# A fused two-graph-layer kernel: its first two and its last three steps rearranged

## The reference, cut to what matters

```python
def reference(x, adj, ...):                      # x [16, 512, 256], adj [16, 512, 512], all float32
    h = maximum(layernorm(x), 0)
    # first graph layer (two hypergraph convolutions over H = (adj != 0)):
    #   conv(x, W, b) = Dn * (H @ (Be * (H^T @ (x @ W^T)))) + b
    #   r = relu(conv(h, W1, b1));  n = layernorm(r) * gamma + beta;  y = conv(n, W2, b2)
    x = x + (y + h)
    h = maximum(layernorm(x), 0)
    # second graph layer (three powers of a transition matrix):
    #   s = h @ Wv + bv;  e = leaky_relu(sj[None, :] + si[:, None] + ab)   (sj, si: s @ aw)
    #   A = adj * exp(e);  T = A / (rowsum(A) + 1e-12)
    #   g = relu(h @ Wk0 + T @ (h @ Wk1) + T @ (T @ (h @ Wk2)) + bk)
    return x + g
```

## Time and profile before

| engine | busy us | share of the span |
|---|---|---|
| TensorE (PE) | 833.2 | 96% |
| its weight loads (PEld) | 769.2 | 89% |
| VectorE (DVE) | 634.1 | 73% |
| ScalarE (ACT) | 475.0 | 55% |
| GpSimd (POOL) | 417.9 | 48% |

### The profile page before, as it was taken

The page is one execution under the profiler, slowest core; times in us unless marked ns, Lnnn a source line. Parts: engine busy times, 40 slices in busy tenths (PEclk is TensorE's granted clock), DMA queues, the critical chain, the costliest instruction groups (busy, mean ns, idle before and its releaser), DMA issues.

```text
span 864.6 us, 16665 instructions
## 1 busy us (share of the span) xinstructions
PE 833.2 (96%) x5822; PEld 769.2 (89%) x5822; DVE 634.1 (73%) x1727; ACT 475.0 (55%) x1001; POOL 417.9 (48%) x586
## 2 busy tenths in 40 slices
PE   8695999999999999999999999999999999999998
PEld 7593998989899898999989899998989999898887
DVE  6875586877868687785868778586877858686645
ACT  4333648365574736656483665648366564835643
POOL 3647154471745547173544727354471735442211
PEclk9788999999999999999999999999999999999999
DMA  8140111304021130402213040211304022020000
GB/s 272 57 131 30 45 65 50 111 16 144 0 83 74 49 109 6 151 0 86 71 49 109 12 146 0 94 64 49 109 11 147 0 86 72 26 74 20 7 25 25
DMA packets 39807, 57.83 MB, mean 67 GB/s; under 512 B 2528, under 2 KB 20960, under 8 KB 39776
## 3 DMA queue, kind: packets, MB, share of 16 engines
q1 hardware_dynamic: 39776, 57.42, 19.9%
HBM read 49.03 MB, written 8.39 MB: 66 GB/s over the span
## 4 chain that ended last, share of the span: by engine, by line
PE 66%; ACT 13%; DVE 10%; issue 3%; POOL 2%; DMA 0%; ACTq 0%; DVEq 0%; POOLq 0%; SPq 0%
PE ps L651 65%; ACT e_sb L557 5%; DVE part_b L1114 3%; ACT e_sb L563 2%; ACT part_a L585 2%; DVE a_lo L1127 2%; DVE e_sb L1121 2%; PE ps L754 2%; POOL part_b L415 2%; ACT p_hi L634 1%; ACT y L580 1%; ACT a_hi L590 1%; DVE st_x L906 1%; ACT part_b L638 1%; DVE hw L914 1%
## 5 line engine op out<-in xcount | busy, mean ns | idle before, releaser
L651 PE MATMUL ps<-w_hi,part_b 128*128 128x256 f32 (+1 forms) x512 | 157.4, 343 | 3.8 <-DVE part_b L933 3.8
L411 POOL TENSOR_TENSOR y<-y,bk_row 128x256 f32<-128x256 f32 x64 | 50.0, 811 | 190.4 <-DVE a_lo L1127 190.4
L651 PEld LDWEIGHTS ps<-w_hi,part_b 128*128 128x128 f32 x512 | 98.0, 191 | 15.7 <-DVE part_b L933 4.2
L415 POOL TENSOR_TENSOR part_b<-xl,part_b 128x256 fp32r<-128x256 f32 x60 | 57.1, 980 | 106.1 <-ACT part_b L638 105.9
L651 PE MATMUL ps<-wk_hi,xt_hi 128*128 128x258 f32 (+1 forms) x256 | 90.0, 352 | 7.9 <-POOL wk_lo L388 6.8
L634 ACT ACTIVATE p_hi<-y 128x256 fp32r<-128x256 f32 x64 | 25.6, 418 | 115.6 <-DVE y L1178 115.6
L651 PE MATMUL ps<-wk_lo,xt_hi 128*128 128x258 f32 (+1 forms) x256 | 87.3, 341 | 0.0
L651 PE MATMUL ps<-wk_hi,xt_lo 128*128 128x258 f32 (+1 forms) x256 | 87.2, 341 | 0.0
L651 PE MATMUL ps<-w_hi,part_a 128*128 128x256 f32 x256 | 77.6, 303 | 8.2 <-DVE part_b L1114 6.2
L1121 DVE TENSOR_TENSOR e_sb<-e_sb,adjt_sb 128x512 f32<-128x512 f32 x64 | 43.9, 685 | 43.7 <-ACT e_sb L563 43.7
L651 PE MATMUL ps<-w_lo,part_a 128*128 128x256 f32 x256 | 73.1, 286 | 0.0
(11 more groups left out here) (140 smaller groups left out, 2517.2 us busy)
## 6 DMA issues: line engine op xcount, KB each, us to landing
adjt_sb<-in_adj_t SPq DMA_DIRECT2D x16, 1024.0 KB, 5.8
adj_sb<-in_adj SPq DMA_DIRECT2D x31, 512.0 KB, 3.4
xin<-in_x SPq DMA_DIRECT2D x15, 512.0 KB, 4.4
out_dram<-x SPq DMA_DIRECT2D x15, 512.0 KB, 3.2
w_row<-in_adj SPq DMA_DIRECT2D x16, 256.0 KB, 3.5
e_sb<-in_w_t SPq DMA_DIRECT2D x2, 512.0 KB, 7.9
y<-in_wk SPq DMA_DIRECT2D x3, 256.0 KB, 6.8
xin<-in_x SPq DMA_DIRECT2D x4, 128.0 KB, 2.2
```

Of the source, the lines that this page charges most:

```text
L411: pool.tensor_tensor(y10[:, t, D:], y10[:, t, D:], bk_row[:, :], ALU.add).then_inc(po_y0, 1)
L415: pool.tensor_tensor(part_b[:, t, D:], g_f[:, t, :], f32(part_b[:, t, 0:D]), ALU.subtract).then_inc(po_glo, 1)
L651: return pe.matmul(dst, stationary, moving, start=first, stop=last, skip_group_check=True)
```

## The change

- FIRST_WAIT goes from 32 to 20.
- Step -1: `w1_lo` on VectorE moves behind the low parts of m.
- Step 0: `w2_lo` moves from GpSimd to VectorE, behind z; the norm of entry 1 moves ahead on VectorE, GpSimd and ScalarE; `inc` tiles 0 and 1 of entry 1 move behind the low parts of the adjacency; `wk_lo` is made here by GpSimd, in two halves, and no longer in step 1.
- Steps 1 to 15: `nb_x` is issued behind the two `u_lo` instructions instead of ahead of them.
- Step 15: v tiles 0 and 1 of entry 14 are taken here, in the other PSUM tensor, between g and o. The norm of x1 of entry 15 is made tile by tile.
- Step 16: v tiles 2 and 3 of entry 14 first; the `keep_clock_up` calls go; ScalarE has an order of its own; p is taken in two phases (row tiles 0 and 1 of A into all four banks, then 2 and 3 bank by bank).
- Step 17: v in the same two phases, with 2 idle products instead of 12. p_lo of step 16 is made by GpSimd, not by VectorE.

```diff
-FIRST_WAIT = 32
+FIRST_WAIT = 20
...
@@ GpSimd, step @@
-                if s.k != 0 and (s.next or s.prev):
+                if s.k != 0 and (s.next or s.here):
                     rs_of_x(s)
                 if s.k == 0:
-                    pool.wait_ge(su_w2hi, 1)
-                    pool.tensor_tensor(w2_lo[:, :, :], w2_f, f32(w2_hi[:, :, :]), ALU.subtract).then_inc(su_w2lo, 1)
+                    rs_of_x(s)
...
-                if s.k == 1:
-                    pool.wait_ge(su_wkhi, 1)
-                    pool.tensor_tensor(wk_lo[:, :, :], wk_f, f32(wk_hi[:, :, :]), ALU.subtract).then_inc(su_wklo, 1)
...
-                if s.prev and s.here:
+                if s.k == 0:
+                    pool.wait_ge(su_wkhi, 1)
+                    for d in range(TD):
+                        pool.tensor_tensor(wk_lo[:, d, :], wk_f[:, d, :], f32(wk_hi[:, d, :]),
+                                           ALU.subtract).then_inc(su_wklo, 1)
+                if s.prev:
                     for t in range(TI):
                         wait(pool, ac_p, at(s, -1, t))
                         pool.tensor_tensor(p_lo[:, t, :], y10[:, t, 0:D], f32(p_hi[:, t, :]),
                                            ALU.subtract).then_inc(po_plo, 1)
+                if s.here and not s.next:
+                    for t in range(TI):
+                        wait(pool, dv_mvx, at(s, 2, t))
+                        pool.tensor_scalar(v_x[:, TI + t:TI + t + 1], mv_x[:, TI + t, 1:2], EPS_LN, 1.0, ALU.add,
+                                           ALU.mult).then_inc(po_vx, 1)
+                        wait(pool, po_vx, at(s, 2, t))
+                        pool.tensor_tensor(rs_x[:, TI + t:TI + t + 1], v_x[:, TI + t:TI + t + 1],
+                                           minus_half[:, 0:1], ALU.pow).then_inc(po_rsx, 1)
@@ ScalarE, step @@
                 xt_of(0)
+                if s.k == 0:
+                    h_of(0)
                 relu(3)
...
+                else:
+                    h_of(1)
+                    h_of(2)
+                    h_of(3)
                 relu_v(0)
...
+                if s.prev and not s.here:
+                    spread(0)
+                    spread(1)
+                    exp(0)
+                    spread(2)
+                    exp(1)
+                    hi_of_a(0)
+                    spread(3)
+                    exp(2)
+                    hi_of_a(1)
+                    exp(3)
+                    hi_of_a(2)
+                    hi_of_a(3)
+                    eps_of_rows()
+                    for t in range(TI):
+                        y10_out(t)
+                    for t in range(TI):
+                        wait(act, dv_p, at(s, -1, t))
+                        act.activation(p_hi[:, t, :], y10[:, t, 0:D], ACT.Copy).then_inc(ac_p, 1)
+                    return
@@ TensorE, step @@
-                if s.prev2 and not s.prev:
-                    wait(pe, ac_y10, at(s, -2))
-                    keep_clock_up(ps1[:, 3, :], 12)
...
-                v_tile(0)
-                v_tile(1)
+                if s.prev2 and s.here:
+                    wait(pe, dv_x1, at(s, -1))
+                    v_tile(s, 0, ps1)
+                    v_tile(s, 1, ps1)
+                elif s.prev2 and s.prev:
+                    wait(pe, dv_x1, at(s, -1, 1))
+                    v_tile(s, 2, ps1)
+                    wait(pe, dv_x1, at(s, -1, 2))
+                    v_tile(s, 3, ps1)
+                elif s.prev2:
+                    wait(pe, ac_y10, at(s, -2))
+                    keep_clock_up(ps1[:, 3, :], 2)
+                    for j in range(2):
+                        wait(pe, po_plo, at(s, -2, j))
+                        for t in range(TI):
+                            v_part(t, j)
+                    for t in range(TI):
+                        for j in range(2, TI):
+                            if t == 0:
+                                wait(pe, po_plo, at(s, -2, j))
+                            last = v_part(t, j)
+                        last.then_inc(pe_v, 1)
...
-                if s.prev and not s.here:
-                    wait(pe, dv_p, at(s, -2))
-                    v_tile(2)
-                    keep_clock_up(ps0[:, 3, :], 10)
...
                 if s.prev and not s.here:
                     wait(pe, dv_sj, at(s, -1))
-                    keep_clock_up(ps0[:, 3, :], 12)
...       (the same two phases for p, with p_part into ps0)
+                if s.here and not s.next:
+                    ahead = Step(4 * s.k + 4, o, s.k + 1, NB)
+                    wait(pe, dv_p, at(s, -1))
+                    v_tile(ahead, 0, ps0)
+                    v_tile(ahead, 1, ps0)
@@ VectorE, step @@
-                    yield
-                    yield
-                    yield
+                    for _ in range(12 if s.k == 0 else 6):
+                        yield
                     dve.wait_ge(po_rsx, at(s, 1))
                     dve.scalar_tensor_tensor(nb_x[:, lo_t:hi_t], mv_x[:, lo_t:hi_t, 0], -1.0, rs_x[:, lo_t:hi_t],
                                              ALU.mult, ALU.mult).then_inc(dv_nbx, 4)
...
+                if s.k == 0:
+                    for _ in chain:
+                        pass
+                    dve.wait_ge(su_w2hi, 1)
+                    dve.tensor_tensor(w2_lo[:, :, :], w2_f, f32(w2_hi[:, :, :]), ALU.subtract).then_inc(su_w2lo, 1)
                 stats_r(2)
...
```

More of the change, by code:

```diff
@@ L471, in x_of @@
                     if s.prev:
+                        if not s.here:
+                            wait(act, dv_nbx, at(s, 1, t))
+                        elif t == 0:
+                            wait(act, dv_nbx, at(s, 1))
                         if t == 0:
-                            wait(act, dv_nbx, at(s, 1))
                             wait(act, *glo(s, -1))
@@ L701, in step, with v_tile @@
                         last.then_inc(pe_u, 2)
-                def v_tile(t):
+                def v_tile(s, t, ps):
                     if s.prev2:
                         for j in range(TI):
[L707 to L711, removed]
+                            if t == 0:
@@ L751, in step @@
                             wait(pe, dv_z, at(s, 0, t))
+                        else:
+                            wait(pe, dv_v, at(s, -2, 1))
+                            wait(pe, ac_xl, at(s, -1, 2 * t + 1))
                         for j in range(2):
@@ L936, in v_tile, with v_out @@
                 def v_tile(t):
+                    if s.prev2 and (s.here or not s.prev or t > 1):
+                        v_out(s, t, ps1)
+                def v_out(s, t, ps):
                     if s.prev2:
@@ L996, in step @@
                     last.then_inc(su_w2, 1)
-                elif s.next or s.prev:
+                    for t in range(TI):
+                        stats_x(t, 1)
                     chain = norm_x()
+                elif s.next or s.here:
+                    chain = norm_x()
+                elif s.prev:
+                    for t in range(TI):
+                        dve.wait_ge(po_rsx, at(s, 1, t))
+                        dve.scalar_tensor_tensor(nb_x[:, TI + t:TI + t + 1], mv_x[:, TI + t, 0:1], -1.0,
+                                                 rs_x[:, TI + t:TI + t + 1], ALU.mult, ALU.mult).then_inc(dv_nbx, 1)
                 total, pos, neg, safe, inv = (dn_t[:, n, :] for n in range(5))
                 next(chain, None)
-                if s.k != -1:
+                if s.k not in (-1, 0):
                     incidence(0)
                 next(chain, None)
-                if s.k != -1:
+                if s.k not in (-1, 0):
                     incidence(1)
@@ L1106, in step @@
                 for _ in chain:
-                    next(chain_x, None)
-                for _ in chain_x:
                     pass
@@ L1225, in step @@
                                           ALU.subtract).then_inc(dv_glo, 1)
+                    ahead = Step(4 * s.k + 4, o, s.k + 1, NB)
+                    v_out(ahead, 0, ps0)
+                    v_out(ahead, 1, ps0)
                 def be_tile(t):
@@ L1272, in step @@
                             dve.bn_stats(st_x[:, TI + t - 1, :], x1[:, q, t - 1, :]).then_inc(dv_st1, 1)
+                        if t > 1 and not s.next:
+                            mean_of_x1(t - 2)
+                    if not s.next:
+                        mean_of_x1(TI - 1)
             run_steps(dve, NB, step)
```

102 lines of the change are left out of this document (54 added, 48 removed).

## The result

The kernel after took 848.9 us (median of four executions, 847.11 to 850.88), the kernel before in the same session 868.5; the ratio is 0.9775, with a 95% interval of 0.976 to 0.979. Forecast were 848.5 us and a range of 842.5 to 855.4. The profiled execution took 848.97 us, its span 847.1 (before 864.6).

The account below looks back on a forecast made before the run. PE's own work bounds the steady loop, so only the ends can move. First steps 15.2, plus 2.2 and 4.1 at the end, less 1.6 for the clock, give 19.9 us: profiled 846.8, median 848.5, range 842.5 to 855.4.

Parts of the forecast that it names:

- What bounds it: Steady loop: only PE's own work sets the time (busy 49.89 of 50.10 us), so only the ends can move.
- First z tile: Step 0: with `w2_lo` off POOL the first z tile comes at about 28.7 instead of 31.21, gain 2.5 us.
- The 0.7 a piece: Step 0: `w2_lo` on DVE would contend with POOL's skip rows, up to 0.7 us a piece.
- z tile to y: Step 0, first z tile to y: 8.6 us instead of 11.04, gain 2.5 us (1.2 to 3.5).
- Step 1: u to z gains 2.0 us, z to y2 6.7 (5.3 with z partly at low clock), full clock afterwards 1.5.
- Step 15 and 16: Up to y2 of step 16: y2 at 831.9 instead of 834.12, gain 2.2 us (0.4 to 3.4).
- p and v of the end: Step 16 from y2 and step 17: v's last tiles end at 858.35 instead of 862.48, gain 4.1 us.
- The clock in step 16: y2 and y10 of step 16 run partly at the low clock, a loss of 1.6 us, called nearly sure.
- Rival (a): The clock holds at both ends: gain 22.5 to 25 us, time 843.4 to 845.9; chance 0.18.
- 26.5 us from y2's start to the last x tile: Step 16 to the end: length of this stretch expected in the profile after, 26.5 us.
- The slower rival: Steps 2 to 15: `nb_x` behind `u_lo` makes PE wait 1.5 us a step, 21 us lost, 870; chance 0.03.

Follow-up runs that it names:

- the kernel with both small edits: The kernel after, plus entry 1's statistics behind the second z tile and four idle products between step 16's transposes: 846.59 us, beside 847.70 for the kernel after.

## Why the prediction was right, and where it was not

The forecast was 0.4 us off, closer than its steps, and that closeness is luck. Between the profiled executions the gain is 17.7 us (the stations add up to 17.5), not 19.9. The rest of the 19.6 between the medians is that the profiled execution of before was 1.8 us under its median and that of after was at its own: I had carried the same distance over to both. So the 2.2 us by which the forecast gain was too large met 1.8 us that came from elsewhere.

- **What bounds it: right.** The middle did not move beyond its own spread, and the gains of the two ends add up.
- **First z tile: the step failed.** "With `w2_lo` off POOL the factors are held only by POOL's four skip tiles" was the error; I had the statistics' load only as the lower bound ("30.2, a gain of 1.0"), and even that was short: 30.63 (a gain of 0.58), and 30.14 and 30.05 in two others. The load waits for POOL's skip tiles, so the edit put an SP transfer in front of the factors, and those tiles themselves ended 4.1 us later than before. Nor did u start some 2 us earlier, but 0.5 (16.00 for 16.51): the first real product came at 9.90, not 8.5, and the second group waited for DVE's `h_lo` until 11.19. The stall itself was read rightly: 2.15 us became 0.16. In the two kernels with the statistics behind z the same instruction ran beside POOL's skip tiles and took 0.51 and 0.70. The Trainium skill (GPSIMD Engine Reference, Specifications) speaks of contention for DVE instructions with two SBUF inputs, and the four numbers agree. The 0.7 a piece that the prediction feared for `w2_lo` on DVE did not come: it took 1.22 at 34.66, POOL being through by 33.94. With the statistics behind z it took 1.21 beside POOL's skip tiles, and these took 3.84 for 2.78.
- **z tile to y: right** (2.32 for 2.5). The stretch repeats to 0.02 us (8.71 to 8.73).
- **Step 1: right in kind, 1.6 too large in size.** `nb_x` gave 1.4 of 2.0; it is the experiment with `nb_x` early that shows this place, by PE's wait of 4.35 for 2.30. `wk_lo` gave 5.7 of 6.7, near the 5.3 written down for a z at the low clock, which is what this execution had. In the kernel after's second profile z ran at full speed and y2 slowly: z to y2 8.75, y2 to p 18.68. So the low clock went to one or the other here, and I had counted it away from both. Of the eleven profiled executions with the new start and `wk_lo` in step 0 it fell on z in four, on y2 in five and on neither in two. One of these two is the kernel with both small edits: its p of step 1 came at 88.74 us, where the forecast had it (103.89 less 15.2), though it needed the earlier z tile for that too.
- **Step 15 and 16: right** (2.16 for 2.2). POOL's chain ran where the forecast had it: from 16.67 to 20.26 us behind p of step 15, for 16.6 to 20.4. Undoing the tile-wise norm alone costs 0.8 of the 2.16.
- **p and v of the end: right** (3.93 for 4.1). From y2 to p it is 10.75 us for 13.00, a gain of 2.25 where 2.3 was forecast (the 12 idle products and ScalarE's order; no run takes them apart), and from p to the last x tile's end 13.68 for 15.36. Without the phases the latter is 15.51, so they are all of it.
- **The clock in step 16: right in size, wrong in certainty.** I took 1.6 off; the fall costs 1.5 and comes in half of the profiled executions. The Trainium skill (TensorE: Matmul & The Clock Gate, Part 4) says that a transpose does not count as busy the same way. From this I had made the fall nearly sure; five of ten held 1.00 over the same transposes, and over the transposes themselves the granted clock was 1.00 in all ten.
- **Two slips of the sums.** Rival (a) adds 1.6 and up to 2.3 to 19.9, which is 21.5 to 23.8, not 22.5 to 25. The sign "26.5 us from y2's start to the last x tile" is 28.36 less 4.1 plus 1.6, so 25.9; it was 24.4 where the clock held and 25.9 where it fell.
- **The slower rival** (`nb_x` late costs each of 14 steps) is refuted: with `nb_x` early the middle takes 705.6 to 706.4 us in four executions, with it late 705.1 to 707.8 in ten, so its place there costs nothing near the 21 us of the rival; a cost or gain under a microsecond would not show.

The errors of the terms had both signs: 3.7 us too much for the start, 1.6 too much off for the clock.

## What to carry to other kernels

When an instruction is moved ahead in a queue, follow what it waits for to the issue of its own load, and what that load waits for: the buffer's last reader on another engine is part of the path. A station gained is not a time gained; after the z tile moved by 3.0 us, y moved by 1.0, because the work taken out of its way stood in the way of the next thing. And hold idle products against the pause they guard over several executions: one profile can show either clock.

## What the runs showed of the hardware

The granted clock is not a function of the program alone: the same instructions with the same pause gave 1.00 or some 3 us at 0.50, and the second low stretch of the start fell on z in one execution, on y2 in the next and on neither in a third kernel with the same waits.

Where a VectorE instruction with two SBUF inputs ran beside GpSimd's additions, one of the two paid, and it was not always the same one. Here it is POOL (statistics behind z, two places):

```profile
16.88 1.35 DVE L1340 TENSOR_TENSOR w_lo<-e_sb,w_hi 128x1024 fp32r<-128x1024 f32 x1
17.11 5.12 POOL L443 TENSOR_TENSOR skip<-xin,b_row 128x256 f32<-128x256 f32 x4
...
31.80 3.84 POOL L382 TENSOR_TENSOR skip<-xin,b_row 128x256 f32<-128x256 f32 x4
```

The four setup skip tiles took 4.15 to 5.12 us in the ten executions with `w1_lo` late in step -1 and the tiles at their place: beside the row sums, and in the longer ones beside `w1_lo` too. With `wk_lo` back in step 1 they started first, at 18.10, and took 2.82, while `w1_lo`, from 19.39, took 2.62 for 1.22. In the kernel before, where `w1_lo` was done by 14.34, they took 2.82 too, and one row sum beside them took 2.15 for 0.69. So `w1_lo`'s new place has a price that the prediction did not have: it puts `w1_lo` beside the tiles that the load of entry 1's x waits for. No run moves `w1_lo` alone, so how much of the first z tile it costs stays open.
